# Block 0 enters attention on its own keys and queries, and the leftovers of the last blocks take other places among the expert tiles

## The reference

```python
scores = einsum('bhnd,bhjcd->bhnjc', q, kc) / sqrt(Dh)     # 4 heads of 32, keys in 8 chunks of 128
scores = clip(scores, -10.0, 10.0)
scores = where(mask == 0, -10.0, scores)
attn = softmax(scores, axis=-1)                            # over the 128 keys of one chunk
ctx = einsum('bhnjc,bhjcd->bhnd', attn, vc)                # the chunks are summed
x = x + layernorm(ctx @ Wo.T + bo + xn) * gamma + beta     # xn = layernorm(x)
...
idx = top_k(xn2 @ Wg + bg, 2)                              # 2 of 8 experts; xn2 = layernorm(x)
x = x + sum over the two of (gelu(xn2 @ W1 + b1) @ W2 + b2)
```

## Time and profile before

| | us |
|---|---|
| median of 3 runs | 810.3 (810.04 to 810.31) |
| profiled execution | 816.87 |
| its span | 815.2 |
| TensorE busy | 707.3 (87%) |
| VectorE busy | 624.4 (77%) |
| ScalarE busy | 491.3 (60%) |
| GpSimd busy | 590.9 (72%) |

### The profile page before, as it was taken

The page is one execution under the profiler, slowest core; times in us unless marked ns, Lnnn a source line. Parts: engine busy times, 40 slices in busy tenths (PEclk is TensorE's granted clock), DMA queues, the critical chain, the costliest instruction groups (busy, mean ns, idle before and its releaser), DMA issues.

```text
span 815.2 us, 17169 instructions
## 1 busy us (share of the span) xinstructions
PE 707.3 (87%) x5435; PEld 367.9 (45%) x5435; DVE 624.4 (77%) x1472; ACT 491.3 (60%) x873; POOL 590.9 (72%) x672
## 2 busy tenths in 40 slices
PE   2588998999999999999999999875767879999994
PEld 1222232333333333333333333231556779999994
DVE  3168899999999999999999999898774545545552
ACT  2266676667667676676666765635434536666663
POOL 5697856979879788798897987969465556445553
PEclk9989999999999999999999999999879989999998
DMA  7100000010110111101100001014212256333330
GB/s 259 51 27 27 1 15 26 14 40 20 34 53 14 40 33 33 40 14 41 53 14 27 20 22 40 14 53 117 61 59 69 87 144 194 104 81 89 107 88 1
DMA packets 45255, 45.43 MB, mean 56 GB/s; under 512 B 7413, under 2 KB 39424, under 8 KB 44720
## 3 DMA queue, kind: packets, MB, share of 16 engines
q1 hardware_dynamic: 38672, 29.47, 12.9%
q0 software_dynamic: 6304, 14.07, 5.0%
q10 hardware_dynamic: 192, 0.80, 0.4%
HBM read 31.46 MB, written 18.34 MB: 61 GB/s over the span
## 4 chain that ended last, share of the span: by engine, by line
PE 35%; DVE 30%; issue 19%; ACT 7%; POOL 4%; SPq 1%; DVEq 1%; DMA 1%; POOLq 0%; ACTq 0%; another core or an unknown queue 0%
DVE e L806 13%; PE scores_ps L535 9%; PE scores_ps L394 7%; DVE ctx_part L814 5%; PE ctx_ps L561 4%; PE z_ps L561 4%; DVE ln_stats L779 3%; ACT e L652 3%; ACT x_rows L657 3%; PE ctx_ps L406 2%; PE job_ps L433 2%; PE z_ps L413 2%; DVE ln_mv L783 2%; DVE best_at L865 2%; PE scores_ps L524 1%
## 5 line engine op out<-in xcount | busy, mean ns | idle before, releaser
L652 ACT ACTIVATE e<-e 128x2048 f32<-128x2048 f32 x128 | 244.6, 1911 | 181.6 <-DVE e L806 181.4
L806 DVE SCALAR_TENSOR_TENSOR e<-scores_ps,bound_mem 128x2048 f32<-128x2048 f32 x128 | 292.3, 2283 | 43.7 <-PE scores_ps L394 43.7
L1200 POOL TENSOR_TENSOR ctx_part<-ctx_part,z_inv 128x1024 f32<-128x1024 f32 x62 | 120.8, 1949 | 65.7 <-DVE z_inv L822 65.7
L1222 POOL DMA_INDIRECT out<-e,near x91 | 89.9, 988 | 93.1 <-issue 52.4
L717 ACT ACTIVATE e<-scores_ps,bound_mem 128x128 f32<-128x128 f32 x364 | 103.8, 369 | 68.0 <-PE scores_ps L535 56.2
L413 PE MATMUL z_ps<-e,one_column 128*32 128x512 f32 x1024 | 134.2, 596 | 0.0
L1212 POOL TENSOR_TENSOR ctx_sum<-ctx_sum,ctx_part 128x512 f32<-128x512 f32 x90 | 115.3, 1281 | 7.2 <-POOL ctx_sum L1212 0.5
L535 PE MATMUL scores_ps<-e,bound_mem 128*128 128x128 f32 x728 | 102.0, 286 | 9.5 <-ACT e L708 4.9
L535 PEld LDWEIGHTS scores_ps<-e,bound_mem 128*128 128x128 f32 x728 | 93.1, 200 | 11.7 <-issue 6.5
L814 DVE STREAM_TRANSPOSE ctx_part<-ctx_ps 128x512 f32<-128x512 f32 x128 | 90.3, 706 | 2.0 <-PE ctx_ps L406 1.6
L1174 POOL DMA_INDIRECT sorted_rows<-x_rows,slot x64 | 63.8, 996 | 22.0 <-issue 21.8
(11 more groups left out here) (156 smaller groups left out, 1009.7 us busy)
## 6 DMA issues: line engine op xcount, KB each, us to landing
near<-sorted_rows SPq DMA_DIRECT2D x91, 130.0 KB
near<-in_x SPq DMA_DIRECT2D x16, 256.0 KB, 2.9
bound_mem<-in_adjT SPq DMA_DIRECT2D x4, 1024.0 KB, 9.3
x_post<-in_x SPq DMA_DIRECT2D x16, 256.0 KB, 2.7
sorted_rows<-sorted_rows SPq DMA_DIRECT2D x12, 130.0 KB
out<-e,near POOLq DMA_INDIRECT x91
sorted_rows<-sorted_rows POOLq DMA_DIRECT2D x10, 130.0 KB
sorted_rows<-x_rows,slot POOLq DMA_INDIRECT x64
```

Source lines behind the costliest of these rows:

```text
L652: nc.scalar.activation(every, every, ACT.Exp, scale=SCORE_SCALE).then_inc(exp_done, 1)
L806: dve.scalar_tensor_tensor(out=e[:, s % E_RING], in0=scores_ps[:], scalar=-CLIP, in1=to, op0=ALU.max, op1=ALU.min).then_inc(clipped, 1)
L1200: nc.gpsimd.tensor_tensor(pair, pair, z_inv[:, v % 2, j:j + 2].to_broadcast([P, 2, SQUARES, DH]), ALU.mult).then_inc(ctx_scaled, 1)
L1222: nc.gpsimd.indirect_dma_start(out=out_rows, out_offset=bass.IndirectOffsetOnAxis(ap=near_u[:, id_at:id_at + 1], axis=0), in_=e_flat[:, at ...
```

## The change

- The loops start at block 0. Ahead of them stand, for block 0, the normalisation, the transposes, keys and queries; values for block 0 and the whole preparation of block 1 are placed in block 0's steps, next to that of block 2. For this, the jobs of blocks 0 to 2 use different banks (`turned_ps`, `k_ps`, `v_ps`, `q_ps`), keys wait for the first drain alone, and queries of block 0 don't wait for the values.
- VectorE's first statistics come before the bias sum. minus_one is computed by ScalarE from minus_half, with a semaphore to `root`.
- SP loads x of block 2 right behind the adjacency.
- The masks: VectorE makes chunks 0 to 3 of the even half and 4 to 7 of the odd half, the latter inside block 0's steps, GpSimd the others, four before block 0 and four in its round.
- `sum_biases` moves from block 15 and the tail's start to block 1, seven sums in steps 0 to 6; b2_pair becomes a tile of its own, and the tiles' ring moves to the end of `near`. SP's loads of tiles no longer wait for ctx_ready.
- SP's last x_post load moves from before the expert weights to behind tile 8's load.
- In block 15 the projection of block 13 is split over steps 1 and 2 as in other blocks, the statistics for it come at step 2, `place(12)` and the counts one step later, the scatter of block 12 is split in two around the residual, and `turn_sum(14)` moves to slot 2.
- In the tail GpSimd scales all of block 15 (`scale_last` goes), and the leftovers are placed anew. The pads start one slot later.

The constants, the banks, SP and TensorE:

```diff
-FIRST = -3
-PAD_LOAD, PAD_SLOT = 28, 22
+PAD_LOAD, PAD_SLOT = 29, 23
+        def rank_ps(v):
+            return job_ps[0] if v == 12 else job_ps[1]
+        def turned_ps(v):
+            return job_ps[1] if v == 1 else job_ps[0]
+        def k_ps(v):
+            return job_ps[1] if v <= 1 else job_ps[0]
+        def v_ps(v):
+            return job_ps[1] if v == 1 else job_ps[0]
+        def q_ps(v):
+            return (ctx_ps, job_ps[1], job_ps[0])[min(v, 2)]
-        b2_pair = near[:, 0:B2_SPAN]
-        xt_at = [B2_SPAN + k * ROW for k in range(XT_RING)]
+        b2_pair = sb("b2_pair", [P, B2_SPAN])
+        xt_at = [6 * SEQ + (k - XT_RING) * ROW for k in range(XT_RING)]
...
+            load_x(2)
...
-            for u in range(FIRST, BLOCKS + 1):
+            for u in range(BLOCKS):
...
-            sp.wait_ge(ctx_ready, STEPS - CHUNKS)
...
+                if i == XT_RING:
+                    load_post(BLOCKS - 1)
...
             def queries(v):
-                pe.wait_ge(v_ready, v + 1)
+                need(pe, v_ready, v + 1 if v else 0)
...
-            for u in range(FIRST, BLOCKS):
+            turn_xn(0)
+            keys(0)
+            queries(0)
+            for u in range(BLOCKS):
                 for j in range(CHUNKS):
...
+                    if u == 0:
+                        if j == 0:
+                            values(0)
+                        if j == 1:
+                            turn_xn(1)
+                        if j == 2:
+                            keys(1)
+                        if j == 3:
+                            turn_xn(2)
+                        if j == 4:
+                            values(1)
+                        if j == 5:
+                            keys(2)
+                            queries(1)
+                        if j == 6:
+                            values(2)
+                        if j == 7:
+                            queries(2)
...
             for k in range(SLOTS):
-                if k == 4:
-                    rank(13)
                 if k == 8:
                     project(15)
-                if k == 9:
+                if k == 10:
                     turn_xn2(14)
-                if k == 11:
-                    gate(14)
-                if k == 13:
+                if k == 12:
                     rank(14)
-                if k == 15:
+                if k == 16:
                     columns(1)
-                if k == 16:
-                    turn_xn2(15)
+                if k == 17:
                     ends(1)
-                if k == 17:
+                if k == 19:
+                    turn_xn2(15)
                     lookup(1)
-                if k == 18:
-                    gate(15)
-                if k == 20:
+                if k == 22:
                     rank(15)
...
                     first_product(k - 1)
+                if k == 2:
+                    rank(13)
+                if k == 10:
+                    gate(14)
+                if k == 20:
+                    gate(15)
                 if k >= 2:
                     second_product(k - 2)
+                if k == 2:
+                    project(14)
```

On ScalarE:

```diff
+            act.wait_ge(half_ready, 1)
+            nc.scalar.activation(minus_one[:], minus_half[:], ACT.Copy, scale=2.0).then_inc(one_ready, 1)
             act.wait_ge(proj_loaded, 16 * 8)
             act.wait_ge(ident_ready, 1)
+            normalise_x(0)
+            drain_xnT(0)
+            drain_k(0)
+            drain_q(0)
+            normalise_x(1)
+            drain_v(0)
...
                 if k < FFN_TILES:
                     drain_turned(k)
+                if k == 6:
+                    normalise_proj(14)
+                if k == 9:
+                    normalise_x2(14)
+                if k == 10:
+                    drain_xn2T(14)
+                    normalise_proj(15)
+                if k == 14:
+                    normalise_x2(15)
+                if k == 20:
+                    drain_xn2T(15)
                 if 1 <= k <= FFN_TILES:
                     gelus(k - 1)
```

On VectorE:

```diff
+            statistics_x(0)
+            dve.wait_ge(bias_filled, 1)
+            dve.scalar_tensor_tensor(out=bo_all[:], in0=job_ps[1][:, 0:1], scalar=float(CHUNKS), in1=bo_sb[:],
+                                     op0=ALU.mult, op1=ALU.add).then_inc(bias_ready, 1)
+            statistics_x(1)
+            for c in range(HALF0_D):
+                prepare_bound(0, c)
+            for u in range(BLOCKS):
...
+                    if s == 0:
+                        statistics_x(2)
+                    if u == 0 and j >= HALF0_D:
+                        prepare_bound(1, j)
...
+                    if u == 1 and j < EXPERTS - 1:
+                        sum_biases(j)
...
             for k in range(SLOTS):
+                if k == 7:
+                    turn_sum(15)
                 if k < FFN_TILES:
                     copy_weights(k)
+                if k == 1:
+                    turn(STEPS - 2)
+                    choose(13)
+                if k == 2:
+                    turn(STEPS - 1)
+                    invert_sums(15)
...
                 if k == 2:
+                    turn_sum(14)
+                    place(13)
+                if k == 3:
                     dve.wait_ge(proj_filled, 15)
...
-                if k in (3, 4):
-                    scale_last(2 * k - 2)
                 if k == 4:
                     add_last(1)
                 if k == 5:
-                    add_last(2)
                     add_last(3)
-                    place(13)
+                    add_last(4)
                 if k == 6:
+                    add_last(6)
...
+                if k >= 2:
+                    add_bias(k - 2)
+                if k == 4:
+                    add_last(2)
+                if k == 5:
+                    add_last(5)
+                if k == 6:
+                    add_last(7)
+                if k == 10:
+                    choose(14)
...
-                if k == 19:
+                if k == 20:
                     choose(15)
-                if k == 21:
+                if k == 22:
                     place(15)
```

On GpSimd:

```diff
+            root(ln["1"], 0)
+            pool_consts()
+            root(ln["1"], 1)
+            prepare_bound(0, HALF0_D)
+            root(ln["1"], 2)
+            for c in range(HALF0_D + 1, CHUNKS):
+                prepare_bound(0, c)
...
-            scale(15, 0)
-            root(ln["2"], 14)
-            scale(15, 2)
-            add_residual(14)
             add_beta(15)
             for k in range(SLOTS):
+                if k == 2:
+                    scale(15, 0)
+                    scatter(13, (0, 1))
+                if k == 3:
+                    scale(15, 2)
+                if k == 4:
+                    root(ln["2"], 14)
+                    scale(15, 4)
+                    scale(15, 6)
+                if k == 5:
+                    add_residual(14)
+                if k == 6:
+                    scatter(13, (2, 3))
                 if k == 7:
                     root(ln["3"], 14)
-                if k in (8, 9):
-                    scatter(13, (2 * k - 16, 2 * k - 15))
+                if k == 8:
+                    root(ln["2"], 15)
                 if k == 10:
-                    root(ln["2"], 15)
-                if k == 11:
                     add_residual(15)
-                if k == 14:
+                if k == 12:
                     root(ln["3"], 15)
```

291 lines of the change are left out of this document (137 added, 154 removed).

## The result

The changed kernel takes 779.05 us (median of 4 runs, 777.06 to 780.37), the kernel before 810.17 beside it (4 runs, 808.65 to 810.31): a ratio of 0.962, 95% interval 0.959 to 0.965, so 31.1 us less. The profiled execution of the changed kernel took 780.4, span 778.7. That is 1.3 above its median, where the profiled execution of before lay 6.6 above its own.

What follows compares the result with a forecast made beforehand. The middle is bound by a VectorE clip and the next four score matmuls waiting for each other; only the ends change. 20.7 - 2.4 - 2.0 + 4.5 + 9.5 + 4.0 = 34.3 off 810.3 gives 776.0 us; range 770 to 783, chance 0.55.

Steps and rivals of the forecast that it cites:

- The start: Preparation before block 0's first scores: scores at 15.7 us instead of 36.4, 20.7 us won.
- the last block: Block 15 up to the first tile's transpose: transpose at 568.0 instead of 572.55, 4.5 us won, ends 0 and 7.
- slots 0 to 12: First tail tiles, block 15's scalings all on GpSimd: 43.3 us instead of 52.8, 9.5 won, ends 0 and 14.
- slots 12 to 28: Middle tail tiles, choices and ranks spaced two slots apart: 4.0 us won of 54.0, ends 0 and 9.
- the last tables: Late tail, last two tables and the pads one slot later: no gain, tile 37 had slots to spare.
- the small rival: At the first exponential: early copy took a set without it, so a second table load of 1.28 us; no chance given.
- Step (b): Block 0's normalisation to first scores: 8.3 us after the shift, scores at 15.7; block 2's rows cost nothing, other end 2.
- (c): Block 0 also carries its values and block 1's preparation: 34.6 us against 32.2, 2.4 lost, other end 6.1.
- (d): GpSimd's eight mask pairs: block 1's ready from 39 to 50 us, block 1 begins at 52; hidden, 2 to spare.
- (e): Bias sums moved to block 1: 2.0 us lost in three steps without a VectorE gap, ends 0.4 and 5.1.
- The first rival: Slots 0 to 28: GpSimd's longer queue eats the gain, 13.5 us more, 789.5 in all; chance 0.17.
- The fourth rival: Tail up to the pads: scalings starve TensorE, clock stays at its lower level, slower, 816 at two thirds; chance 0.03.

Runs made afterwards that it cites:

- the like profile: Kernel before the change, no edit, run and profiled a second time: measured 808.1 us (ratio 0.9996), profiled execution 807.0.
- the three scatters: Against the combined kernel with later adds: pick back behind the transpose, three block 12 scatters ahead of GpSimd's scaling, one behind the residual; 784.0 us, ratio 0.961.

## Why the prediction came out as it did

Forecast 776.0, measured 779.05, inside the likeliest case (770 to 783). The start was right in its mechanism. Behind it the total is partly luck: against the like profile the last block, slots 0 to 12 and slots 12 to 28 won 13.0 for 18.0, the last tables lost 3.3 for nothing, and two of these terms rest on a false step.

**The start** was right step by step. Scores at 15.00 for 15.7: the first were at the full clock already, and the keys at 2.07 as taken. ScalarE loaded a table once at the start; the next load is the gelu's at 555.45. The Trainium skill, ScalarE: Activation LUTs, section "Table sets: the hidden batching unit", has copy and identity in every set; the trace agrees that none was loaded anew at the first exponential, so the small rival of 1.28 us didn't come. Block 1's first clip came at 51.74 for 52. Step (b) took nothing for block 2's rows, with 2 as the other end: its landing time was right (20 for 20.3), but the step let the statistics follow a clip that ends at 20, and that clip ended at 18.6, since the scores were early. So what the start had won beyond its forecast went into this wait, 1.8 us, and the low clock behind it. (c) lost 3.3 for 2.4 with it, in this trace; in others with the same start it lost 0.5 to 3.6. (d) held: GpSimd's last mask operation ended at 51.45, forecast 50, ahead of block 1, and no clip waited for one. (e) lost 1.8 for 2.0; what it saved in block 15 was 1.7 by the trace, for the 3.3 of four sums (which take 3.6 in the trace of before).

**The last block** came to 4.0 us for 4.5, but by a false sum. The clips were to take 31.6 us and took 35.2. The failed step is the list of steps, 4.4 for the one that now holds the pick: I moved the row count out of GpSimd's way because the earlier trace rows show it at 1.69, and didn't ask what else of that kind would move in. The pick did, from a place beside a root, where it takes 1.3, to one beside a scaling and a residual, where it takes 5.3; with GpSimd's part cut the steps sum to 31.3. Luck made up for it: 3.3 us came behind the last clip, where the forecast had left 5.5 us (568.0 less a last clip at 562.5) for GpSimd's queue and the normalisation. The first tile follows the last clip by 2.4 us, not 5.7. That is the load's new place and not the bias sums: with three sums put back there it follows by 2.4 too, and with the old order of loads and no sums by 5.8, of which it waits 2.79 for the load.

**Slots 0 to 12**: 9.5 forecast, 7.9 against the like profile and 7.9 against the old placement on the new start. The mis-sized term is the turned sum: it came at 581.1, 29.7 us behind the first tile, forecast 26 (594 less 568). The like profile has 31.4 and the old placement 31.3, so the four scalings on GpSimd brought it only 1.7 us sooner. Most of the 7.9 stands behind it, where normalisations, ranks and choices were placed anew: slots 10 and 11 took 6.8 us for 10.5. The first rival, that GpSimd's longer queue takes all of this, fell; but sharing the scalings moved the sum by 1.0 us only, so GpSimd's queue alone isn't the bound. Whether VectorE's, with its held copies and adds, is as long, or TensorE's order, stays open: moving the adds behind the copies only moved the wait.

**Slots 12 to 28**: 4.0 forecast, 1.2 to 1.4 won. The failed step is the base, "54.0 us for 30.4 of tiles and 4.4 of leftovers" with waits of 4.5 to be saved. 10.7 us of it were pauses and the low clock behind them in the one profiled execution. I had noted that this execution lay 6.6 above the median and took the surplus off at the end as one number; it had to be asked in which stretch it lay, since a gain read from that stretch is inflated by it.

**The last tables and pads**: "no gain there, and tile 37 had slots to spare" is the step that failed, with 8.4 us against the first profile and 3.3 against the like one. The slots to spare in the first profile were there because TensorE was late. Two pads behind a load make SP slower (3.9 us) than the tiles (1.9), in the kernel before as in the changed one. Part of the 3.3 is this execution's: behind its wait of 2.26 us the clock fell for 3.4 us, and two traces with the same pads in which it didn't (the bias sums put back, and the moved pick) took 21.3 and 21.4 us for slots 28 to 36, near the like profile's 21.0.

**The fourth rival**, a slow clock through the tail, didn't come: 0.96 and 1.00 granted up to slot 28. In single executions the clock does fall there, as the first profile of before and that of the three scatters show, by some 10 us and not 60.

## What to carry to other kernels

- A small operation on VectorE is priced by what GpSimd does beside it, not by its size. Before you move one, list GpSimd's queue at the new place: 28 numbers took 0.15 us beside a root and 3.0 to 3.7 beside a scaling and the product behind it.
- Where the profiled execution lies off the median, find the stretch that holds the surplus before you take a gain from that stretch, and look there for pauses without a releaser as well as for the clock; a second profile of the kernel before is worth more than a finer sum.
- Work added to a queue that must keep ahead (loads with pads between) is compared in its rate with its consumer at full speed, not with the pace that a stalled profile shows.
